# First layer's scores with the keys on the partitions, ahead of the maxima taken from scores with the queries there

## What is computed

```python
q = (query @ Wq.T + bq).reshape(Bt, St, H, D).transpose(0, 2, 1, 3)     # D = 8
k = (key @ Wk.T + bk).reshape(Bt, -1, H, D).transpose(0, 2, 1, 3)
scores = jnp.einsum('bhqd,bhkd->bhqk', q, k) / math.sqrt(D)
scores = jnp.where(mask, scores, neg_inf)
attention = jax.nn.softmax(scores, axis=-1)
out = jnp.einsum('bhqk,bhkd->bhqd', attention, v)
return out.transpose(0, 2, 1, 3).reshape(Bt, St, E) @ Wo.T + bo
```

## Time and profile before

| | us |
|---|---|
| median of three runs | 279.56 |
| the runs | 279.52, 279.56, 281.11 |
| profiled execution | 278.56 |
| its span, first to last instruction | 276.7 |
| busy in the span: PE, DVE, ACT, POOL | 254.6, 207.6, 187.1, 138.4 |
| mean granted TensorE clock | 0.984 |

### The profile page before, as it was taken

One profiled execution on the slowest core, in us unless ns is written; L12 is line 12 of the kernel. 1 busy time (PEld: TensorE's weight loads), 2 busy tenths in 40 slices (PEclk: granted clock), 3 DMA queues, 4 the chain that ended last, 5 costly groups with the idle time before them and its releaser, 6 DMA issues. The chain is left out here.

```text
span 276.7 us, 6465 instructions
## 1 busy us (share of the span) xinstructions
PE 254.6 (92%) x1909; PEld 202.6 (73%) x1909; DVE 207.6 (75%) x593; ACT 187.1 (68%) x395; POOL 138.4 (50%) x209
## 2 busy tenths in 40 slices
PE   7798999999698999997999999999979998789994
PEld 5475766677566687786777888777767776789993
DVE  3989679778987697788578777777798514786673
ACT  3379779878677687784866767678776553666462
POOL 7305710204125075754465485448847794926380
PEclk9979999999799999999999999999999999999998
DMA  6568375200032656644574766766532041200530
GB/s 200 192 178 284 131 267 137 55 4 2 0 70 60 142 121 148 135 104 107 135 184 113 179 174 171 194 162 160 141 82 60 24 136 38 85 33 28 189 112 19
DMA packets 25984, 32.88 MB, mean 119 GB/s; under 512 B 4000, under 2 KB 18144, under 8 KB 25824
## 3 DMA queue, kind: packets, MB, share of 16 engines
q1 hardware_dynamic: 25520, 32.27, 43.4%
q10 hardware_dynamic: 432, 0.22, 0.3%
HBM read 14.32 MB, written 3.47 MB: 64 GB/s over the span
## 5 line engine op out<-in xcount | busy, mean ns | idle before, releaser
L1220 PE MATMUL bank<-ident,probs 128*128 128x128 f32 x512 | 79.7, 279 | 3.1 <-ACT probsT L757 1.3
L1220 PEld LDWEIGHTS bank<-ident,probs 128*128 128x128 f32 x512 | 59.3, 143 | 20.5 <-issue 15.9
L596 POOL TENSOR_SCALAR probs<-probs,rsum 128x512 f32<-128x512 f32 x64 | 44.2, 693 | 49.7 <-DVE rsum L945 49.6
L757 ACT ACTIVATE probsT<-bank 128x512 f32<-128x512 f32 x77 | 45.7, 593 | 24.3 <-PE bank L1220 24.3
L936 DVE CUSTOM_DVE_ANT_0 masked<-bank,mask 128x512 f32<-128x512 f32 x64 | 43.8, 684 | 18.7 <-PE bank L1352 17.0
L744 ACT ACTIVATE probs<-masked,neg_max 128x512 f32<-128x512 f32 x64 | 44.4, 722 | 8.0 <-DVE neg_max L936 6.0
L1379 PE MATMUL bank<-probsT,val 128*32 128x256 f32 (+1 forms) x512 | 46.6, 384 | 0.9 <-ACT mixT L768 0.9
L749 ACT ACTIVATE probs<-masked,neg_max 128x512 f32<-128x512 f32 x64 | 46.0, 719 | 1.6 <-DVE neg_max L936 1.6
L936 DVE CUSTOM_DVE_ANT_0 masked<-bank,shared 128x512 f32<-128x512 f32 x64 | 42.4, 685 | 5.0 <-PE bank L1345 4.9
L952 DVE COPY probsT<-bank 128x512 f32<-128x512 f32 x51 | 34.9, 684 | 6.7 <-PE bank L1220 6.4
L1379 PEld LDWEIGHTS bank<-probsT,val 128*32 128x32 f32 (+1 forms) x512 | 24.9, 123 | 18.0 <-issue 5.1
(11 more groups left out here) (244 smaller groups left out, 546.8 us busy)
## 6 DMA issues: line engine op xcount, KB each, us to landing
k_both<-k_low SPq DMA_DIRECT2D x32, 128.0 KB, 2.6
k_both<-k_high SPq DMA_DIRECT2D x32, 128.0 KB, 2.7
q<-q_split SPq DMA_DIRECT2D x32, 128.0 KB, 2.4
probsT<-staged_gate SPq DMA_DIRECT2D x32, 128.0 KB, 3.0
q<-q_split SPq DMA_DIRECT2D x32, 64.0 KB, 2.0
parts<-staged_k SPq DMA_DIRECT2D x7, 256.0 KB, 2.7
w_flat<-in_w SPq DMA_DIRECT2D x1, 1536.0 KB, 8.0
staged_k<-k_high SPq DMA_DIRECT2D x2, 512.0 KB, 3.2
```

The source lines that it names most:

```text
L596: pool.tensor_scalar(p, p, rsum[:, u % NCOL:u % NCOL + 1], 1.0, ALU.mult, ALU.mult).then_inc(normed, 1)
L757: act.activation(probsT[:, k.m % 2, h, :, qt * P:qt * P + P], turn_bank[u % 2][:, :].rearrange("p (k q) -> p k q", q=P), ACT.Copy).then_in ...
L1220: ins = pe.transpose(dst[0:rows, t * P:t * P + P], src, ident[:, :])
```

## The change

It treats the 56 units of blocks 1 to 7 ("crosswise") in another way; block 0 and the second layer keep theirs.

- **Scores of such a unit stay**, but VectorE now only takes the row's maximum from them (into `nm`; the other output is not read). They stand further ahead: 15 steps, and for units 8 to 23 two in each step from 1 to 8 (`scores_at`). No scores are issued in steps 49 to 57.
- **gather(k)**, once a block, on VectorE: the eight columns of maxima are split in a high and a low part and turned by a 32x32 transpose. **stage_rows(k)**, on SP: one transfer writes them to DRAM, and after it has landed eight transfers bring them as rows into the fourth row of q0's groups (q's fourth combination is given up for it; k has ones there). So the matmul subtracts the maximum.
- **cross(u)** on TensorE, first in its step: a bf16 matmul with the identity brings the mask, turned (`maskT`), into a turn bank, 512 columns; two fp32r matmuls of 256 columns add scores with 128 keys on the partitions and 256 queries. **exp_crossed(u)** on ScalarE reads the bank and writes `probsT`. The turn, the copy and the first exponential fall away for these units.
- ones and zeros for the fourth row are filled by POOL and written to DRAM by two transfers; another transfer loads the mask turned. DVE makes a bf16 identity.
- The second batch's norm and jobs move forward: ln 11 to 4, kn 13 to 3, qn 14 to 6, v0 15 to 8. Copies of block 0 go half to each engine. probs has five slots in the first layer, the sixth holds maskT. The fifth split of w1 waits for the last cross.

```diff
-LN01_AT = 6
+LN01_AT = 0
+CROSS_AT = BLOCKS[1].first
+CROSS_LEAD = 15
+def scores_at(u):
+    return max(u - CROSS_LEAD, 1 + (u - CROSS_AT) // 2) if crosswise(u) else u - LEAD
+GATHERS = {scores_at(k.end - 1) + 1: k for k in BLOCKS[1:8]}
...
+            def stage_rows(k):
+                n = k.m - 1
+                sp.wait_ge(gathered, n + 1)
+                sp.dma_start(staged_rows[k.m % 2], rows_turned[:, :]).then_inc(rows_staged, 16)
+                sp.wait_ge(rows_staged, 16 * (n + 1))
+                if k.m >= 3:
+                    sp.wait_ge(crossed, BLOCKS[k.m - 2].end - 1 - CROSS_AT)
+                src = staged_rows[k.m % 2].rearrange("(i l h t) c -> l h t i c", i=4, l=4, t=NQ)
+                for h in range(4):
+                    for low in range(2):
+                        p = 32 * h + 4 * low + 3
+                        sp.dma_start(q0[p:p + 1, k.m % 4, h, :].bitcast(F32).rearrange("p (t i c) -> p t i c", t=NQ, i=4),
+                                     src[low, h:h + 1]).then_inc(rows_loaded[k.m % 2][h], 16)
...
             stage_k0(1)
+            stage_rows(BLOCKS[1])
             stage_q0(1)
+            stage_rows(BLOCKS[2])
             for k in BLOCKS[4:8]:
                 stack_k0(k)
                 stack_q0(k)
+                if k.m >= 5:
+                    stage_rows(BLOCKS[k.m - 2])
+            stage_rows(BLOCKS[6])
+            stage_rows(BLOCKS[7])
...
+            def exp_crossed(u):
+                k, h, half = unit(u)
+                act.wait_ge(crossed, u - CROSS_AT + 1)
+                if k.m >= 2:
+                    act.wait_ge(mixed, k.m - 1)
+                act.activation(probsT[:, k.m % 2, h, 2 * half:2 * half + 2, :],
+                               turn_bank[u % 2][:, :].rearrange("p (k q) -> p k q", q=SQ),
+                               ACT.Exp, scale=float(k.depth) ** -0.5).then_inc(cross_exped, 1)
...
+            def gather(k):
+                n = k.m - 1
+                high, low = row_parts[:, 0:8], row_parts[:, 8:16]
+                dve.wait_ge(maxed, scored_block(k))
+                step(dve.tensor_copy(high, nm[:, k.m % 2, :]))
+                step(dve.tensor_tensor(low, nm[:, k.m % 2, :], high.bitcast(F32), ALU.subtract))
+                if n:
+                    dve.wait_ge(rows_staged, 16 * n)
+                dve.transpose(rows_turned[:, :], row_parts[:, :].bitcast(F32)).then_inc(gathered, 1)
...
+            def cross(u):
+                k, h, half = unit(u)
+                dst = turn_bank[u % 2]
+                if half == 0:
+                    pe.wait_ge(rows_loaded[k.m % 2][h], 32 * ((k.m + 1) // 2))
+                if u < CROSS_AT + 2:
...
+                else:
+                    pe.wait_ge(cross_exped, u - CROSS_AT - 1)
+                pe.matmul(dst[:, :], ident_b[:, :], maskT[:, 2 * half:2 * half + 2, :], start=True, stop=True, skip_group_check=True)
+                for n in range(2):
+                    c = (2 * half + n) * P
+                    ins = pe.matmul(dst[:, n * SQ:n * SQ + SQ], k0[:, k.m % 4, c:c + P], q0[:, k.m % 4, h, :],
+                                    start=False, stop=True, skip_group_check=True)
+                ins.then_inc(crossed, 1)
...
             def attend(t):
-                if 0 <= t + LEAD < TOTAL:
-                    scores(t + LEAD)
+                if crosswise(t):
+                    cross(t)
+                for u in S_AT.get(t, ()):
+                    scores(u)
...
-                if 0 <= t < TOTAL:
+                if 0 <= t < TOTAL and not crosswise(t):
                     turn(t)
```

## The result

| | before | after |
|---|---|---|
| median, us (four runs of each) | 279.88 | 293.72 |
| lowest to highest | 279.52 to 281.11 | 290.27 to 294.54 |
| profiled execution, its span | 278.56, 276.7 | 290.27, 288.5 |
| mean granted TensorE clock | 0.984 | 0.976 |

After over before is 1.046, with a 95% interval of 1.037 to 1.055 (the medians alone give 1.049). In all that follows a run that is more than 1.5% longer than the fastest of its kernel counts as slow and is left out of the ratios, while medians are over all runs. I had said 283.8 (276.5 to 290), slower the likeliest: the direction held, the size did not. The profiled execution of after is the quickest of its four; its span is 11.8 us above the one of before, and that difference is taken apart here. The other runs lie 3.3 to 4.3 us higher, and their mean granted clock is lower (0.957 to 0.963, not 0.976).

The account below looks back on a forecast made before the run. VectorE and ScalarE were taken to set the first layer's plain step, TensorE the second layer; 9.5-6.1+0.1+0.7 = +4.2 on the profiled 278.56 gave 282.8, and 1.0 more for the median 283.8, range 276.5 to 290.

Parts of the forecast that it names:

- SyncE's eight row loads: SP's queue, after each block's maxima are written to DRAM: eight loads at 0.43 us of issue each.
- The front: Steps 1 to 8, with maxima made ahead on VectorE: step 9 starts at 35.6 us against 26.09, +9.5.
- The step: Plain first-layer step on TensorE, scores plus cross: 0.76 us, between 0.59 and 0.88.
- Rival (b): Plain step: every change of matmul kind is exposed, step 0.88, +9.7, 289.3 us; chance 0.15.
- rival (d): Plain step: bf16 streams at half the price, step 0.59, kernel faster by 3.6, 276.0 us; chance 0.15.
- Steps 9 to 48: First layer's 40 steps with mixes, jobs and waits: 44.6 us against 50.7, -6.1.
- the quantisation: Steps 44 and 45: VectorE's quantisation holds scores up; 0.5 us of it kept, as VectorE has room.
- The wait at step 17: Scores(32) waits 2.1 us for block 4's operands, issued behind block 2's row loads in SP's queue.
- Rival (c): SP's queue is cheap: issues of 0.33 and landings of 1.5 us give 279.3 us; chance 0.20.
- Steps 49 to 57: Only cross on TensorE, but SP's row issues delay scores(64): 14.2 us against 14.1, +0.1.
- From scores(64) on: Steps 58 to 63: cross at 0.47 us where a turn was 0.35, six times, +0.7.
- Rival (e): Transposes really cost their busy time, 279 ns each, so removing turns gives 252.7 us; chance 0.05.

Follow-up runs that it names:

- the filler: Changed kernel plus unread matmuls, two in each of steps 1 to 8 and fourteen in step 17: ratio to before 1.045.
- whole rows: Changed kernel with each of the eight row loads a block one contiguous 1 KB row in DRAM, not eight 128 B pieces: 284.44 us.
- the early jobs alone: Kernel before, with only the second batch's norm and jobs moved to the changed kernel's steps (ln 4, kn 3, qn 6, v0 8): 277.89 us, ratio 0.995.

## Why the prediction was right in direction and short in size

The step that failed is the price of SyncE's eight row loads: 0.43 each, bounded by 0.33 and 0.44, where they take 0.63, 5.0 a block and not 3.4. The front was short too, by 2.8, through waits of VectorE and the first gather. With the loads whole the time is 284.4, close to the forecast 283.8, but in part by luck: there the front's excess and the cheaper step offset each other. The terms one by one, in the profiled executions:

**The step.** I took 0.76 between bounds of 0.59 and 0.88; it is 0.70, the sum of the fp32r rows. Rival (b), every change of kind exposed (0.88), and rival (d), bf16 at half the price (0.59), both fall by the step as a whole. Nothing like the 0.20 against 0.12 of the earlier trace rows is left in it; a long matmul stands ahead of each change. This error was to the good: 40 x 0.06 = 2.4.

**Steps 9 to 48.** Now 40 x 0.70 = 28.0, mixes 9.4 and jobs 2.2 make 39.6. Waits: 4.1 at scores(32), 0.9 for the rows of block 4, 1.3 and 1.0 in steps 44 and 45 where the quantisation stands: 7.3. Behind the 4.1, from scores(32) to cross(19), 4.6 us pass (50.60 to 55.2); with the clock held up by the filler the same work takes 3.1 (53.68 to 56.76): 1.5 for the clock. That is 48.4 of 49.7, and 1.3 stay unaccounted. Against my 44.6 the miss is -2.4 for the step, +2.0 for the wait (4.1, not 2.1), +1.5, +0.9, +1.8 for the quantisation (I kept 0.5) and the 1.3. The quantisation was simply misjudged: I reasoned that VectorE had room, but the waits in these two steps, for VectorE's maximum, are 1.29 and 1.01 in after and were 1.28 and 1.04 before, 2.3 each time.

**The wait at step 17** is the mis-sized term that matters. I named place and cause, and priced eight loads at 0.43, the row of the first q operand loads. They take 0.63. A piece count was in the diff (an inner rearrangement into 2 x 4 pieces), and my bound from both sides, 0.33 to 0.44, was too narrow, since it came from transfers of another form. Seven blocks by 1.6 us more make 11 us of SyncE's time; what reached the end of the profiled execution is not that sum but the wait in step 17 (2.0 more than forecast), the clock behind it, the 0.9, and 2.3 in front of scores(64). Rival (c), SP is cheap, took 0.33 a load and 279.3. With whole rows a load costs less than that, 0.29, and the time is 284.4: the cheap queue alone doesn't bring 279.3, with the front as it is.

**Rows at 9.9.** The run without them shows 5.8 of this at scores(64) (102.91 to 97.11), as the spans do (288.5 to 282.8). The other 4 us lie in the difference of the medians from the profiled runs: after's is 3.4 above its profiled run, the other's 0.8 below. The clock goes with it: after's runs have 290.27 at a mean granted 0.976 and 293.5 to 294.5 at 0.957 to 0.963, the other's 283.10 at 0.976 and 284.62 at 0.962. At the same 0.976 the rows cost 7.2, near 0.96 some 8 to 9. Where in the run the other executions lose their clock is not known. How late the first write lands also differs from profile to profile (3.05 and 5.58 with the same transfers ahead), which would give such a spread; that it does is not shown.

**The front.** Forecast +9.5, measured +12.3. The start is later by 0.63 (0.8 forecast). The first gather takes 1.43, not 0.6: the cast of 8 columns into fp32r alone is 0.69, where later ones take 0.17. VectorE waits 3.5 us between 20 and 38 us, where I allowed 1.5: 0.8 for scores and 0.85 for the products of v0, which TensorE issues at 0.54 to 0.61 of its clock, 0.6 for q and k from ScalarE, and 1.24 for the scores that stand behind cross(8) and its wait for rows. The two together are 2.8, the whole miss. The clock is in them: at a granted 1.00 the stretch up to the first gather is 1.5 shorter, as said above. I had named the clock among the bounds (up to 2 us for each fall) and left it out of the sum. Of my 1.5, 0.7 was for the row's landing; cross(8) does wait 0.62 for it, and yet the run without rows, at its lower clock, is at step 9 no earlier. Part of the front comes back, as the early jobs alone show: 1.3 behind at the first mix, 0.9 ahead at the second.

**Steps 49 to 57.** I had +0.1 and it is +0.7, by the same term of 0.63 for 0.43: SyncE issues the rows of block 7 from 91.08 to 96.19, and scores(64) waits 2.3. With whole rows this wait is 1.6 and with none 0.8.

**From scores(64) on** I had +0.7 for the six crosses of steps 58 to 63, and it is -0.2 (185.6 against 185.8). The first of the six stands ahead of the mark, and the exchange costs less than the 0.12 I took for each: from scores(65) to scores(66) 1.63 us pass (105.87 to 107.50) where before has 1.59 (93.80 to 95.39), since the scores matmul behind cross costs 0.23 (105.87 to 106.10) and behind a turn 0.31 (93.80 to 94.11). The rest of the second layer and the experts take as long as before.

Rival (e), that a turn is worth its 279 ns a matmul, falls too: with front and rows both gone the exchange brings 3.8 us (277.89 to 274.09; some 5 by the ratios, 0.995 and 0.977, as the two were measured apart), not 36. The Trainium skill, "TensorE: Matmul & The Clock Gate", section on the PE-mode transpose, gives some 275 ns for a transpose (in bf16) and speaks of it as a duration. The trace agrees on the size, with 279 in the earlier trace rows; four of them stand in 0.35 us in the earlier trace rows, so the duration is not what one costs.

## What to carry over

Before a score matrix is computed twice to spare a transpose, price the second use's precondition: here the exchange itself gained 4 to 5 us, the front with the maxima ahead of it and the clock lost there cost 9.8, and their way through DRAM 9.9. Take a queue's issue time from a row of the same form, with its pieces and partitions, and not from the nearest size; and look at what is queued behind them; a layout that makes each piece whole can be worth more than fewer transfers. And a small write whose landing is waited for should not stand behind a megabyte in the same queue.

## What the runs showed of the hardware

- SyncE's issue time of a transfer depends on its form more than on its bytes. From start to start: 0.29 us for one row of 1 KB, 0.63 for the same 1 KB in eight pieces, 0.60 for two rows of 1 KB, 0.44 for 32 KB on 32 partitions.
- A 16 KB write to DRAM landed in 1.4 to 2.0 us with nothing large ahead of it, 2.7 to 5.6 behind 2.1 MB issued some 6 to 8 us earlier, and 7.3 behind the same issued from 2.2 us earlier.
- A bf16 matmul of 512 columns and two fp32r ones of 256, together, cost 0.46 us from start to start, as three fp32r ones of these widths would (0.23 + 0.12 + 0.12), with two changes of kind among them.
- VectorE operations on 128 x 8 numbers with an fp32r output took 0.17 us each in six gathers of after, and 0.69 and 0.53 in the one beside which GpSimd was busy.
- TensorE's granted clock fell to between 0.50 and 0.67 for 4 us or more in the front of most profiles here (before: 0.66 from 16 to 20), and the work from the first maximum to the first gather then took 1.5 to 2.2 us longer. Only the kernel without rows and front kept 1.00 from 12 to 44 us. Filler matmuls held the granted clock at 1.00 through a wait of 4 us, and gained nothing that these runs can show, since the wait was for data.
